# Attention pipelines without steady-state filler matmuls, with late steps moved back and the expert router's opening moved in

## The reference

```python
x = _layernorm(x + _L0_attn_ref(x, ...))            # window of 16 either side; row 0 attends to all
x = _layernorm(x + _L0_xattn_ref(x, ctx_512, ...))  # causal self attention + attention to ctx, one projection
x = _layernorm(x + _L0_ffn_ref(x, ...))             # expert choice, 16 experts
x = _layernorm(x + _L1_attn_ref(x, ...))            # gated recurrence and MLP
x = _layernorm(x + _L1_xattn_ref(x, ctx_512, ctx_512, ...))
x = _layernorm(x + _L1_ffn_ref(x, ...))             # top-2 mixture of 8 experts
```

```python
rms = jnp.sqrt(jnp.mean(xf * xf, axis=-1, keepdims=True) + EPS)
xn = xf / rms * norm_weight
logits = xn @ router_weight.T + router_bias
_, idx = jax.lax.top_k(logits.T, top_k)
```

## Time and profile before

| | us |
|---|---|
| median of 3 runs | 622.6 |
| lowest, highest | 620.65, 623.71 |
| the profiled execution | 616.85 |
| its span | 615.1 |
| its mean granted clock of PE | 0.922 of 2.4 GHz |

### The profile page before, as it was taken

The page is one execution under the profiler, slowest core; times in us unless marked ns, Lnnn a source line. Parts: engine busy times, 40 slices in busy tenths (PEclk is TensorE's granted clock), DMA queues, the critical chain, the costliest instruction groups (busy, mean ns, idle before and its releaser), DMA issues. The chain is left out here.

```text
span 615.1 us, 10513 instructions
## 1 busy us (share of the span) xinstructions
PE 503.2 (82%) x3848; PEld 239.5 (39%) x3848; DVE 382.2 (62%) x876; ACT 221.5 (36%) x447; POOL 182.3 (30%) x296
## 2 busy tenths in 40 slices
PE   3899988878989898852499957885998889789994
PEld 2445443333333333320159843363333333334441
DVE  7646756577675768147965678644478842255574
ACT  2213452454656556701012115222117654332221
POOL 7736365644473622125000025101434000000000
PEclk9999998999999999977789978896899986799998
DMA  6321012235411100025040022000311000425200
GB/s 229 89 61 52 4 52 55 69 114 165 140 54 52 36 19 3 3 67 243 2 138 2 2 66 89 0 2 14 90 52 53 4 3 0 143 64 150 58 17 18
DMA packets 26899, 38.03 MB, mean 62 GB/s; under 512 B 3648, under 2 KB 19520, under 8 KB 26464
## 3 DMA queue, kind: packets, MB, share of 16 engines
q1 hardware_dynamic: 26848, 37.36, 20.0%
HBM read 23.91 MB, written 0.59 MB: 40 GB/s over the span
## 5 line engine op out<-in xcount | busy, mean ns | idle before, releaser
L1052 DVE TENSOR_REDUCE nmax<-bank 128x2 f32<-128x512 f32 (+2 forms) x240 | 145.6, 625 | 80.6 <-PE bank L832 38.3
L940 ACT ACTIVATE arena<-bank 128x512 f32<-128x512 f32 (+2 forms) x256 | 130.0, 524 | 136.0 <-PE bank L836 94.6
L498 PE MATMUL bank<-causal_qk,identb 128*128 128x512 bf16 x309 | 99.6, 428 | 28.9 <-DVE moe_top L1330 16.0
L836 PE MATMUL bank<-arena 64*128 64x256 bf16 (+2 forms) x512 | 87.0, 262 | 1.6 <-ACT arena L940 1.5
L832 PE MATMUL bank<-arena 62*128 62x256 bf16 (+2 forms) x512 | 85.2, 258 | 3.6 <-DVE nmax L1052 3.2
L877 PE MATMUL bank<-arena 128*32 128x256 f32 (+4 forms) x1088 | 75.3, 356 | 7.2 <-ACT arena L940 4.4
L832 PEld LDWEIGHTS bank<-arena 62*128 62x128 bf16 x512 | 30.1, 95 | 67.5 <-issue 49.3
L498 PEld LDWEIGHTS bank<-causal_qk,identb 128*128 128x128 bf16 x309 | 28.4, 107 | 69.2 <-issue 42.8
L702 POOL TENSOR_SCALAR_AFFINE_SELECT arena<-arena 128x256 f32<-128x256 f32 x64 | 25.5, 407 | 55.8 <-ACT arena L940 55.1
L836 PEld LDWEIGHTS bank<-arena 64*128 64x128 bf16 x512 | 30.6, 95 | 19.6 <-issue 9.7
L877 PEld LDWEIGHTS bank<-arena 128*32 128x32 f32 x1088 | 21.6, 110 | 34.2 <-issue 20.1
(11 more groups left out here) (284 smaller groups left out, 819.5 us busy)
## 6 DMA issues: line engine op xcount, KB each, us to landing
arena<-arena SPq DMA_DIRECT2D x96, 128.0 KB, 2.4
fcw<-in_fc1T SPq DMA_DIRECT2D x16, 256.0 KB, 3.1
arena<-in_fc2T SPq DMA_DIRECT2D x1, 4096.0 KB, 15.1
arena<-comb_rows SPq DMA_DIRECT2D x16, 256.0 KB, 5.2
fcw<-in_last SPq DMA_DIRECT2D x1, 2304.0 KB, 8.5
arena<-pos_rows SPq DMA_DIRECT2D x16, 128.0 KB, 2.9
arena<-comb_rows SPq DMA_DIRECT2D x16, 128.0 KB, 4.6
w<-in_w SPq DMA_DIRECT2D x1, 1216.0 KB, 6.2
```

The source lines that it names most:

```text
L498: nc.tensor.matmul(bank[:, :], m.identb[:, :], m.causal_qk[:, 0:4, :], start=True, stop=True)
L836: sins = t.matmul(sout[i], stack_rows(m, nh, h, 1, SCORE_ROWS)[:, i * P:(i + 1) * P], stack_rows(m, nh, h, 0, SCORE_ROWS)[:, spans[i][0]:s ...
L940: s.activation(m.prob[h % 8][:, 0:w], score_bank(n, h)[:, 0:w], ACT.Exp).then_inc(exps, 1)
L1052: v.tensor_reduce(m.nmax[n % 2][:, qt, h0:h0 + nh], MX[c % NMX][:, 0:nh * (k1 - k0)].rearrange("p (h k) -> p h k", h=nh), AX.X, ALU.max, n ...
```

## The change

Three things change together.

**Late steps by job.** The offsets 59, 61, 63, 67 become a tuple: `NEAR` keeps them, `FAR` is 60, 63, 65, 70. Layer 0's first job is `NEAR` (the first causal job needs its result), all others, and all of layer 1, are `FAR`. The router's steps in layer 1 follow `FAR.x1t`, and its combination transpose goes from slot 99 to 101.

```diff
-S_X1T = 67
-S_OTT, S_YT = 59, 61
+Chain = namedtuple("Chain", "ott yt out x1t")
+OTT, YT, OUT, X1T = range(4)
+NEAR, FAR = Chain(59, 61, 63, 67), Chain(60, 63, 65, 70)
...
+    steps = [NEAR if tight and n == 0 else FAR for n in range(NJ)]
...
+        def late(slot, step, more=0):
+
+            found = [n for n in range(NJ) if start[n] + steps[n][step] + more == slot]
+            return found[0] if found else None
...
-S_COMB = 99
+S_COMB = 101
```

```diff
-                    keep_warm(nc, m, M0, F_OTT)
+                    keep_warm(nc, m, M0, F_OTT if n == NJ - 1 else 0)
...
-                    keep_warm(nc, m, M0, F_YT)
+                    keep_warm(nc, m, M0, F_YT if n == NJ - 1 else 0)
...
                         if nm == 0:
                             pe.wait_ge(high_in, 1)
-                        keep_warm(nc, m, MX[c % NMX], fill if nm == 0 else F_STACK)
+                            keep_warm(nc, m, MX[c % NMX], fill)
                         pe.wait_ge(stack[nm % 4], 16 * TERMS * (nm // 4 + 1))
...
-                        keep_warm(nc, m, score_bank(nh, h), F_SHIFT)
+                        keep_warm(nc, m, score_bank(nh, h), F_SHIFT if nh in (0, NJ - 1) else 0)
```

```diff
+S_NORM_COL = 140
+S_OPENING = [16 * (5 + 2 * b) + FAR.out + 4 for b in range(BATCH)]
...
+            if slot == first:
+                dve.wait_ge(self.x1_ready, BATCH + b + 1)
+                link(v.tensor_tensor(self.sq[:, :, :], x2, x2, ALU.mult))
+                link(v.tensor_reduce(self.ms[:, ts], self.sq[:, :, :], AX.X, ALU.add))
+                v.tensor_scalar(self.ms[:, ts], self.ms[:, ts], 1.0 / D, MOE_EPS, ALU.mult, ALU.add).then_inc(self.ms_ready, 1)
+            if slot == first + 2:
+                dve.wait_ge(self.rs_ready, b + 1)
+                v.tensor_tensor(m.x[1][:, ts, :], x2, self.rms[:, ts].unsqueeze(2).broadcast_to([P, QT, D]),
+                                ALU.mult).then_inc(self.xs_ready, 1)
```

More of the change, by code:

```diff
@@ L10 @@
 from concourse import mybir
+from collections import namedtuple
 from contextlib import ExitStack
@@ L633, in _ @@
             for slot in range(slots):
-                if side:
-                    side.sync(sp, slot)
+                for part in sides:
+                    part.sync(sp, slot)
                 n = at(slot, S_SHIFT + 1)
@@ L966, in _ @@
             for slot in range(slots):
-                if side and slot:
-                    side.vector(dve, slot)
+                for part in sides:
+                    if slot:
+                        part.vector(dve, slot)
                 if dve_first and slot == S_SPLIT:
```

199 lines of the change are left out of this document (115 added, 84 removed).

## The result

The changed kernel takes **628.9 us** (median of four runs, 626.5 to 632.7), beside 621.9 for the kernel before on the same chip, 1.1% more; the measured ratio is 1.028, interval 1.019 to 1.037. It is slower, though by how much is open: of 89 further runs of before (median 622.9) 17 are as long as the fastest of these four. The forecast of 608.1 was wrong in its sign. The profiled execution took 629.7 us with a span of 628.0; that of before had 616.85 and 615.1.

A forecast was written before the change was run, and what follows sets the result against it. TensorE was taken as nearest to full, with GpSimdE pacing about 207 to 218 us. Terms -8 - 6.5 - 3.5 - 4.9 + 2.4 + 6 = -14.5 us, against the 622.6 us median, gave 608.1 us; range 596 to 622.

The forecast's parts named there:

- Step 1: Fillers at 0.22 us each: layer 0 loses 88 (19.4 us of TensorE time), layer 1 loses 24 (5.3 us).
- Step 3: Layer 0's real gain from fillers and covered waits: 8 us up to 130 us, 6.5 us from there on.
- Rival D: Fillers never cost anything, each standing before a wait as long: 616 us; chance 0.22 together with another rival.
- GpSimdE sets the pace: Layer 0's causal stretch, about 207 to 218 us: GpSimdE's unbroken queue limits it, however fast TensorE is.
- the prediction's own sign: Causal stretches shrinking as much as local ones would show that GpSimdE was not the pace.
- Step 2: Late steps in the attention pipeline: nearly 6 us of waits for ot and y covered, about 3.2 for x, none for yT.
- Step 4: Layer 1's attention pipeline: 3.5 us gained from fillers and waits, ends 1 and 7.
- Step 5: Expert stage's opening, last x to first MAX8: 5.2 us left of about 10, a gain of 4.9 us.
- Step 6: Opening work of three batches placed among layer 0's jobs: 0.8 us lost each, 2.4 us in all.
- Step 7: TensorE's clock: two more short falls to the low level, 6 us lost; ends 8 gained and 33 lost.
- these idle moments join up: Causal stretch: with fewer fillers and waits, TensorE stands 1.6 and 2 us before products with V, risking clock falls.
- Rival B: Clock stays low for long in layer 0's four causal stretches and layer 1's tail: slower, 635 us with five falls; chance 0.15.

The follow-up runs named there:

- e2: The kernel before without the steady fillers, late steps and opening unchanged: 629.6 us, ratio 1.033.
- e3: The kernel before without the steady fillers and with the late steps, opening left in the expert stage: 618.7 us, ratio 1.016.
- e5: The kernel before with the late steps, all fillers kept: 618.8 us, ratio 1.014.
- e11: Layer 0 as in the kernel before, layer 1 as in the changed kernel (no steady fillers, late steps), opening not moved: 617.6 us, ratio 1.011.
- e4: The changed kernel with the late steps back at their old slots for all jobs: 625.2 us, ratio 1.026.
- e6: The kernel before with only the opening moved, fillers and old steps kept: 620.3 us, ratio 0.996.
- e1: The changed kernel with all steady fillers put back: 622.0 us, ratio 1.019.
- e14: e12 plus the opening's move: 610.9 us, ratio 0.988.
- e8: The changed kernel with GpSimdE's power of the opening queued behind its slot's mask instead of ahead: 630.6 us, ratio 1.035.
- e12: e11 with layer 0's steady fillers moved, four each ahead of the waits for ot, y and x: 606.9 us, ratio 0.982.

## Why the prediction was wrong, step by step

*Step 1, the fillers' own time.* 88 and 24 fillers at 0.22 us was right as TensorE time.

*Step 3, what of it comes true.* Wrong in size and reason. The forecast took 14.5 us out of layer 0; the profiles give 6.8 for the fillers (e2) and nothing for the late steps, +1.4 (e3: 285.1 us with 73.7 low). I saw at one place that nothing is waited for behind three fillers and took it for the rule; two thirds of the fillers' time came back as waits elsewhere. Rival D, with 4 us for layer 0, was nearer to what was left (5.4), though its own reason, that fillers never cost anything, does not hold either: 6.8 of 19.4 us were real. The reason given was not borne out: "GpSimdE sets the pace" asked for mask waits of 5 us or more, and after has 1.4 (3.5 in the whole kernel). The timeline of GpSimdE in after, where the masks of causal job 8 begin:

```profile
212.73 0.80 POOL L805 TENSOR_SCALAR_AFFINE_SELECT arena<-arena 128x256 f32<-128x256 f32 x2 [6.77 <-ACT arena L1043]
...
217.33 0.79 POOL L805 TENSOR_SCALAR_AFFINE_SELECT arena<-arena 128x256 f32<-128x256 f32 x2 [1.85 <-ACT arena L1043]
```

The row at 217.33 us is the one that stands at 207.03 in the earlier trace rows. From there GpSimdE is unbroken again, for 9 us against 11, and TensorE meets no wait for a mask in that time, though this is inside the fall from 217 us, where TensorE itself is slow. The 6.8 us of waiting for ScalarE lie ahead of the stretch, and before has them too (7.2 us at 202.66). So an unbroken row of work on an engine does not show that others stand for it. e2 says the same: between ScalarE's copies of `ot`, less 0.318 for each us low, its causal jobs are 2.8, 0.6 and 0.6 us shorter than before's and one 0.3 longer, its local jobs 0.5, 0.6 and 0.8 shorter. So without the fillers causal stretches shrank at least as much as local ones, which was the prediction's own sign that GpSimdE was not the pace. In after, which has the late steps and the opening too, the local jobs are 0.5, 1.9 and 1.0 shorter (not 2 each), and the causal ones 0.0 to 1.8 longer.

*Step 2, the late steps.* Right for `ot` and for most of `x`. Wrong for `y`, whose wait was to be covered: it is 2.4 us with the late steps alone (e5, before 1.8) and 4.4 in after. Wrong for `yT` too, which was to stay at 4.0 us and went. I did not ask what stands next to the new slots: the output product came one slot ahead of the shift's transposes in bank 7 (`z`, 6.3 us), and TensorE, past `ot`, ran into ScalarE at the scores (12.2 us).

*Step 4, layer 1.* -3.5 forecast, -3.5 measured at the full clock. That the figures are equal is in part luck: the same layer gives -5.4 and -5.5 in e3 and e11. There are also 22 us less at the low clock, which I had not looked for. That part varies between profiles (10 to 36 us low over all of them, whatever their fillers).

*Step 5, the opening.* 5.2 us forecast from the last `x` to MAX8, 5.0 measured. The timeline of VectorE (before: the earlier trace rows):

```profile
296.85 0.60 DVE L1136 TENSOR_SCALAR x<-z,mv,rstd 128x128 f32<-128x128 f32 x2 [1.13 <-POOL rstd L826]
297.48 0.43 DVE L527 TENSOR_TENSOR open_sq<-x 128x256 f32<-128x256 f32 x1
...
299.44 0.42 DVE L532 TENSOR_TENSOR x<-x,open_rms 128x256 f32<-128x256 f32 x1 [0.87 <-POOL open_rms L480]
302.48 1.22 DVE L1392 MAX8 moe_top<-hid 16x8 f32<-16x1024 f32 x1 [2.62 <-PEq L661]
```

*Step 6, what it costs among the jobs.* 2.4 forecast, with 4.5 as its end. Measured in layer 0 at the full clock: 1.9 (e4 against e2), 3.7 (after against e3), and with fillers 5.3 to 6.0 (e6, e1 against e5, e14). The opening was moved for nothing.

*Step 7, the clock: the step that decided the sign.* 6 us forecast, 18 to 23 measured: 58 us more at the low clock by the medians, 73 by the profiles. The price of a us at the low clock was set somewhat high (0.41, and 0.318 by the runs); the number and the length of the falls were what failed. I had seen that "these idle moments join up" and counted two short falls more than before's two in layer 0; there were eleven, three of them of 14 to 27 us. What misled me was the row 135 to 140 us: a stretch with a third idle that did not fall, but it had fillers around it. Rival B named the course and its places (the clock stays low through causal stretches although TensorE works, as its 21 busy us of 24 at half clock show), gave it 0.15, and put 33 us on it. That it is the thinness of that work which keeps the clock low is not shown by a run of its own: from 217 to 241 us maxima ran beside the scores, as B's doubt had it, and the clock stayed low all the same. Its other doubt, "the fall after 102 us was over in 6.9", came from a kernel that still had its fillers. The Trainium skill (TensorE: Matmul & The Clock Gate, "A second HAM failure mode: psum-queue depth-cycling") tells of a kernel in which TensorE idles shortly but often between groups of matmuls and its clock goes up and down; this trace agrees, with waits of 1.1 to 1.9 us ahead of ten of the eleven falls.

What stays open: why the clock falls in one run and not in another of the same kernel (89 runs of before, 68 to 151 us low), what the opening among the jobs does to the clock (e3 to after, e8), and what the longer queue of the late steps costs apart from `z`.

## What to carry to other kernels

A filler's worth is its cost at its place against the low-clock time it saves; price both, from the trace and from runs at different clocks. Fillers belong ahead of a wait that TensorE really meets, after everything they themselves must wait for, and none where the clock holds without them. When a step is moved in a schedule written by slots, look at what uses the same bank in the next slot, not only at the wait it leaves.

## What the hardware did that I had not expected

One core alone spreads by 28 us over 89 runs of one kernel, and nearly all of it goes with the granted clock (0.881 to 0.944): with that taken out by the line, 1.1 us are left (standard deviation). In after's profile the clock stayed low for 24 us while TensorE was busy for 21.3 of them, and for 27 more at the end of layer 0, where scores and products with V were most of its work. And two kernels with about the same number of filler matmuls (e11 and e12: 88 and 92 in 50 to 262 us), and the same work, differ by 11 us at the median, by where those stand.
